# Row sums of a projection: summed on VectorE and multiplied by ones, in a two-block attention kernel on one core

## What is computed

```
# first block: softmax attention, D = 64
q = einsum('bcn,dc->bnd', x, Wq) + bq
k = einsum('bcn,dc->bdn', ctx, Wk) + bk
v = einsum('bcn,dc->bdn', ctx, Wv) + bv
x = einsum('bcm,bnm->bcn', v, softmax(q @ k)) + x
# second block: no softmax, CI = 256
g_x     = conv1x1(g_w, g_b, ctx)^T
theta_x = conv1x1(theta_w, theta_b, x)^T
phi_x   = conv1x1(phi_w, phi_b, ctx)
W = theta_x @ phi_x / 1024
wy = conv1x1(w_w, w_b, (W @ g_x)^T)
out = bn_gamma * (wy - bn_mean) / sqrt(bn_var + eps) + bn_beta + x
```

## Time and profile before

| | |
|---|---|
| Time, median of 3 runs | 1041.94 us (1041.92 to 1042.0) |
| Span of the profiled execution | 1041.2 us, first to last instruction |
| Median less span | 0.7 us |
| Granted TensorE clock | 1.000 |
| Busy: TensorE, VectorE, ScalarE, GpSimd | 99%, 62%, 47%, 26% |
| Instructions | 13910 |

### The profile page before, as it was taken

One profiled execution on the slowest core, in us unless ns is written; L12 is line 12 of the kernel. 1 busy time (PEld: TensorE's weight loads), 2 busy tenths in 40 slices (PEclk: granted clock), 3 DMA queues, 4 the chain that ended last, 5 costly groups with the idle time before them and its releaser, 6 DMA issues.

```text
span 1041.2 us, 13910 instructions
## 1 busy us (share of the span) xinstructions
PE 1032.8 (99%) x5119; PEld 854.6 (82%) x5119; DVE 647.8 (62%) x923; ACT 490.6 (47%) x843; POOL 274.9 (26%) x235
## 2 busy tenths in 40 slices
PE   8999999999999999999999999999999999999998
PEld 6778888888888887888878888888887888878887
DVE  6994467844588355873558736586365863658625
ACT  7652564436553264533744337453275532655321
POOL 1312351122601236012350124401244012430220
DMA  7536152451424524245242442434433344323512
GB/s 253 162 75 204 63 196 49 106 190 62 162 56 108 181 67 157 61 111 173 81 142 68 112 166 91 132 76 111 158 109 114 82 121 143 123 101 81 130 33 82
DMA packets 80915, 122.06 MB, mean 117 GB/s; under 512 B 13136, under 2 KB 46672, under 8 KB 80848
## 3 DMA queue, kind: packets, MB, share of 16 engines
q1 hardware_dynamic: 71632, 104.39, 32.9%
q10 hardware_dynamic: 9216, 16.78, 5.1%
HBM read 70.79 MB, written 16.78 MB: 84 GB/s over the span
## 4 chain that ended last, share of the span: by engine, by line
PE 95%; DVE 2%; SPq 1%; DMA 1%; ACT 1%; issue 0%; DVEq 0%; ACTq 0%
PE pG L651 34%; PE pG L546 15%; PE pG L662 8%; PE pG L554 5%; PE pG L587 5%; PE pT L684 4%; PE pG L684 4%; PE pG L561 4%; PE pT L493 3%; PE pS L599 2%; PE pS L482 2%; PE pM L630 2%; PE pM L639 2%; PE pT L599 2%; SPq L396 1%; PE pG L567 1%
## 5 line engine op out<-in xcount | busy, mean ns | idle before, releaser
L651 PE MATMUL pG<-pt,vT 128*128 128x512 f32 x1536 | 353.9, 389 | 0.0
L651 PEld LDWEIGHTS pG<-pt,vT 128*128 128x128 f32 x1536 | 286.8, 188 | 58.6
L1063 POOL TENSOR_TENSOR xms<-xr,xms 128x512 fp32r<-128x512 f32 x64 | 89.7, 1401 | 324.6 <-ACT xms L840 324.6
L546 PE MATMUL pG<-wv,x2s 128*128 128x512 f32 x720 | 168.6, 391 | 0.0
L546 PEld LDWEIGHTS pG<-wv,x2s 128*128 128x128 f32 x720 | 134.0, 188 | 30.3 <-issue 2.6
L996 DVE SCALAR_TENSOR_TENSOR xr<-pG,cl,xr 128x512 f32<-128x512 f32 x64 | 47.9, 749 | 170.2 <-PE pG L651 170.2
L840 ACT ACTIVATE xms<-xr 128x512 fp32r<-128x512 f32 x64 | 40.3, 629 | 178.5 <-DVE xr L996 178.5
L967 DVE TENSOR_TENSOR pt<-mv,pt 128x512 fp32r<-128x512 f32 x128 | 90.2, 756 | 39.5 <-ACT pt L811 39.3
L1059 POOL TENSOR_TENSOR ys<-yf,ys 128x256 fp32r<-128x256 f32 x32 | 28.9, 906 | 295.5 <-ACT ys L802 295.5
L811 ACT ACTIVATE pt<-mv 128x512 fp32r<-128x512 f32 x128 | 71.9, 620 | 37.5 <-PE pM L639 27.9
L662 PE MATMUL pG<-xms,wth 128*128 128x512 f32 x384 | 88.3, 389 | 0.0
(11 more groups left out here) (138 smaller groups left out, 1433.7 us busy)
## 6 DMA issues: line engine op xcount, KB each, us to landing
mv<-tp SPq DMA_DIRECT2D x512, 64.0 KB, 2.0
x2T_f<-in_ctx2T_dram SPq DMA_DIRECT2D x32, 512.0 KB, 4.8
xr<-in_x_dram ACTq DMA_DIRECT2D x64, 256.0 KB, 4.6
st<-in_ctx_dram SPq DMA_DIRECT2D x31, 512.0 KB, 5.5
st<-in_x_dram SPq DMA_DIRECT2D x29, 512.0 KB, 4.0
out_dram<-oh SPq DMA_DIRECT2D x32, 256.0 KB, 2.2
out_dram<-xr SPq DMA_DIRECT2D x31, 256.0 KB, 7.7
x_raw<-in_x_dram SPq DMA_DIRECT2D x3, 512.0 KB, 8.0
```

The lines of the kernel that those rows point to most:

```text
L546: last = mm(bank, x2s[:, l, c, 128 * m:128 * m + 128], wv[:, r, c, :], start=(c == 0 and n == 0), stop=(c == 3 and n == 2))
L651: last = mm(bank, vT[:, l, m, 128 * c:128 * c + 128], pt(h)[:, r, m, :], start=(m == 0 and n == 0), stop=(m == 7 and n == 2))
L1063: done(tt(xms(h)[:, c, LO, :], xr[c][:, :], xms(h)[:, c, HI, :].bitcast(F), ALU.subtract), "xlo")
```

## The change

The projection that is added as a term of rank one becomes that of phi, not of g, so that it is needed as a row that is the same on all partitions. It is made in three steps.

1. `acc` (blocks 1 to 7, VectorE): `acc = 8 phi_b + sum over c and part of wpg[:, part, c, 0:256] * scol[:, c]`, eight scalar_tensor_tensor of 256 columns, each of which waits for the one before. In block 0 the same is done on GpSimd, which has a tensor_scalar and a tensor_tensor for each of the eight, and one tensor_scalar for the bias.
2. `acc` on ScalarE makes the HI part, `accl` on VectorE (GpSimd in block 0) the LO part.
3. `psi` (TensorE): two matmuls with a 128 by 128 matrix of ones add up the 128 partitions, which leaves the row in all of them, in `pM[:, 1, 256:512]`. ScalarE copies it to `psi_row` after Y:3, and `mt` multiplies it by the column of g_b.

`s`, `gs`, `gt`, `gsum` and their tiles go. `Y` is made with phi_w^T (the first 256 columns of `wpg`) and phi_b. In `M` the operands change sides: `wpg` is loaded and `ys` moves. `mtf` and `mts` are moved to the place of `gram` and `xms0`; `T:4` therefore waits for `M:1`, and the evacuation PV:0,3 for `B:1`. In the strings of blocks 1 to 7 `T:4` stands ahead of `mts` and `T:5` ahead of PV:0,0, on ScalarE and VectorE, and `tr:7` ahead of `mt`. In block 0 the copy of `w_w` waits for `psi`, since the tiles of the sum lie at its place.

```diff
 LATER = dict(
     pe=(
-        "k:0 k:1 q:0 q:1 v:0 v:1 gs v:2 S:0 S:1 L:0 L:1 L:2 gt S:2 S:3 L:3 G:0 G:1 G:2 GT:0 G:3 GT:1 S:4 S:5 v:3 "
+        "k:0 k:1 q:0 q:1 v:0 v:1 psi v:2 S:0 S:1 L:0 L:1 L:2 S:2 S:3 L:3 G:0 G:1 G:2 GT:0 G:3 GT:1 S:4 S:5 v:3 "
...
+        psi_row = at("psi_row", [128, 256], F, rd + 8192)
+        mtf = at("mtf", [128, 2, 256], F, rd + 10240)
+        mts = at("mts", [128, 2, 2, 256], R, rd + 12288)
...
-                        last = mm(bank[:, 0:256], gram[:, l, d, 128 * c:128 * c + 128], wpg[:, r, d, 256:512],
+                        last = mm(bank[:, 0:256], gram[:, l, d, 128 * c:128 * c + 128], wpg[:, r, d, 0:256],
...
-            def do_gs(b):
-                eng.wait_ge(s_wlo, W_PG + 1)
-                wait(eng, "slo", b)
+            def do_psi(b):
+                wait(eng, "acclo", b)
                 if b:
                     wait(eng, "Blo", b - 1, 1)
                 else:
+                    eng.wait_ge(s_ones, 1)
                     wait_free(eng, b, 3)
-                for c in range(4):
-                    for part in (HI, LO):
-                        last = mm(pM[0:2, 1, 256:512], sst[:, c, :], wpg[:, part, c, 256:512],
-                                  start=(c == 0 and part == HI), stop=(c == 3 and part == LO))
-                done(last, "s_row")
...
+                    wait(eng, "GTlo", b, 1)
+                for part in (HI, LO):
+                    last = mm(psi_bank, ones_r[:, :], accs(b)[:, part, :], start=(part == HI), stop=(part == LO))
+                done(last, "psi")
...
-                        last = mm(pM[:, k, 0:256], ys[:, l, c, 128 * k:128 * k + 128], wpg[:, r, c, 0:256],
+                        last = mm(pM[:, k, 0:256], wpg[:, l, c, 256 + 128 * k:384 + 128 * k], ys[:, r, c, :],
...
+            def do_acc(b):
+                wait(eng, "acc", b, 7)
+                done(act(accs(b)[:, HI, :], acc(b)[:, :], ACT.Copy), "acchi")
...
                 if t == 4:
-                    wait(eng, "B", b, 1)
+                    wait(eng, "M", b, 1)
...
+            def do_acc(b):
+                wait(eng, "x2sum", b, 3)
+                eng.wait_ge(s_br8, 1)
+                for n in range(8):
+                    c, part = divmod(n, 2)
+                    if n:
+                        wait(eng, "acc", b, n - 1)
+                    done(stt(out=acc(b)[:, :], in0=wpg[:, part, c, 0:256].bitcast(F), scalar=scol[:, c:c + 1],
+                             in1=acc(b)[:, :] if n else br[:, 256:512], op0=ALU.mult, op1=ALU.add), "acc")
...
+            def do_acc(b):
+                wait(eng, "x2sum", b, 3)
+                eng.wait_ge(s_wlo, W_PG + 1)
...
+                    eng.tensor_scalar(accp[:, :], wpg[:, part, c, 0:256].bitcast(F), scol[:, c:c + 1], None,
+                                      ALU.mult).then_inc(s_accp, 1)
+                    eng.wait_ge(s_accp, n + 1)
+                    done(tt(acc(b)[:, :], accp[:, :], acc(b)[:, :] if n else br[:, 256:512], ALU.add), "acc")
```

More of the change, by code:

```diff
@@ L572, in do_GT @@
                 wait_free(eng, b, use_g(b, r))
-                if r == 0:
-                    wait(eng, "s_colc", b)
                 for c in range(r + 1, 4):
@@ L708, in do_w @@
                 eng.wait_ge(s_wd[i], 16)
+                if i == W_O:
+                    wait(eng, "psi", 0)
                 act(w_split(i, HI), W_RAW[i], ACT.Copy).then_inc(s_whi, 1)
@@ L793, in do_G @@
                 wait_free(eng, b, use_g(b, r))
+                if b and r >= 2:
+                    wait(eng, "psi", b)
                 done(act(gram[:, HI, r, G_FROM[r]:512], gram_f[r][:, G_FROM[r]:512], ACT.Copy), "Ghi")
@@ L797, in do_GT @@
                 wait(eng, "GT", b, r)
+                if b:
+                    wait(eng, "psi", b)
                 done(act(gram[:, HI, r + 1:4, 128 * r:128 * r + 128], gram_turned(r), ACT.Copy), "GThi")
@@ L812, in do_T @@
                 done(last, "Thi")
-            def do_gs(b):
-                wait(eng, "qlo", b)
-                wait(eng, "s_row", b)
-                done(act(grow, pM[0:2, 1, 256:512], ACT.Copy), "s_rowc")
-            def do_gt(b):
-                wait(eng, "s_col", b)
-                done(act(gsc[:, :, :], pM[:, 0, 384:388].rearrange("p (k i) -> p k i", i=2), ACT.Copy), "s_colc")
             def do_mts(b):
@@ L839, in do_PV @@
                 wait_free(eng, b, G_PV + 4 * h + c)
+                if h == 0 and c == 3:
+                    wait(eng, "B", b, 1)
                 done(act(xms(h)[:, c, HI, :], xr[c][:, :], ACT.Copy), "xhi")
@@ L849, in _ @@
             do = dict(w=do_w, xr=do_xr, x2=do_x2, x2a=do_x2a, xs=do_xs, x1=do_x1, k=do_k, q=do_q, k2=do_k2, q2=do_q2, v=do_v, S=do_S, L=do_L, G=do_G,
-                      GT=do_GT, Y=do_Y, x2T=do_x2T, s=do_s, T=do_T, gs=do_gs, gt=do_gt, mts=do_mts, B=do_B, xc=do_xc, PV=do_PV,
+                      GT=do_GT, Y=do_Y, x2T=do_x2T, acc=do_acc, psi=do_psi, T=do_T, mts=do_mts, B=do_B, xc=do_xc, PV=do_PV,
                       th=do_th)
@@ L970, in do_mt @@
             def do_mt(b):
-                wait(eng, "s_colc", b)
                 wait(eng, "M", b, 1)
-                if b == 0:
-                    eng.wait_ge(s_nbg, 1)
+                wait(eng, "psirow", b)
                 for k in range(2):
-                    done(stt(out=gsum[:, k:k + 1], in0=gsc[:, k, 0:1], scalar=nbg[:, k:k + 1], in1=gsc[:, k, 1:2],
-                             op0=ALU.add, op1=ALU.add), "gsum")
-                for k in range(2):
-                    wait(eng, "gsum", b, k)
-                    done(stt(out=mtf[:, k, :], in0=br[:, 0:256], scalar=gsum[:, k:k + 1], in1=pM[:, k, 0:256],
+                    done(stt(out=mtf[:, k, :], in0=psi_row[:, :], scalar=gb(k), in1=pM[:, k, 0:256],
                              op0=ALU.mult, op1=ALU.add), "mtf")
@@ L1051, in do_x2T @@
                 done(tt(x2Ts[:, LO, m, :], x2T_raw(b, m), x2Ts[:, HI, m, :].bitcast(F), ALU.subtract), "x2Tlo")
-            def do_s(b):
-                wait(eng, "shi", b)
-                done(tt(sst[:, :, LO], scol[:, :], sst[:, :, HI].bitcast(F), ALU.subtract), "slo")
+            def do_acc(b):
+                wait(eng, "x2sum", b, 3)
+                eng.wait_ge(s_wlo, W_PG + 1)
+                eng.wait_ge(s_bd, 16)
+                eng.tensor_scalar(br[:, 256:512], br[:, 0:256], N / 128.0, None, ALU.mult).then_inc(s_br8, 1)
+                eng.wait_ge(s_br8, 1)
+                for n in range(8):
+                    c, part = divmod(n, 2)
+                    if n:
+                        wait(eng, "acc", b, n - 1)
+                    eng.tensor_scalar(accp[:, :], wpg[:, part, c, 0:256].bitcast(F), scol[:, c:c + 1], None,
+                                      ALU.mult).then_inc(s_accp, 1)
+                    eng.wait_ge(s_accp, n + 1)
+                    done(tt(acc(b)[:, :], accp[:, :], acc(b)[:, :] if n else br[:, 256:512], ALU.add), "acc")
+                wait(eng, "acchi", b)
+                done(tt(accs(b)[:, LO, :], acc(b)[:, :], accs(b)[:, HI, :].bitcast(F), ALU.subtract), "acclo")
             def do_Y(b, c):
```

69 lines of the change are left out of this document (36 added, 33 removed), and 18 rows, old and new, of tables (act, dve, pe).

## The result

| | before | after |
|---|---|---|
| Time, median | 1041.97 us (1041.92 to 1042.54) | 1053.16 us (1052.74 to 1054.57) |
| Ratio | | 1.0107, 95% interval 1.0094 to 1.0119 |
| Span of the profiled execution | 1041.2 us | 1050.9 us |
| Start of k in block 1 | 140.5 us | 146.7 us |
| Mean length of a block, start of block 1 to start of block 7 | 128.24 us | 128.76 us |

What follows compares the result with a forecast made beforehand. TensorE was taken as the bound, busy 1032.8 of 1041.2 us. Block 0's cost of 1.0 less 5.3 gained in blocks 1 to 7 gave -4.3 us, so 1037.6 us, with range 1035.6 to 1040.4.

Steps and rivals of the forecast that it cites:

- TensorE's work, blocks 1 to 7: TensorE, blocks 1 to 7: matmuls 0.70 us less and small transposes 0.21 less, a gain of 0.91 us a block.
- stall in blocks 1 to 7: TensorE before S:0, blocks 1 to 7: waits 0.15 us a block because VectorE's sum delays q.
- block 0: Block 0: GpSimd's sum and its operations alongside VectorE's cost 1.0 us in all, at least 0.3, at most 3.5.
- the meeting: VectorE's sum, blocks 1 to 7: running beside GpSimd's x2T:0 split costs 0.9 us once a block.
- the upper bound of 62: GpSimd, block 0: latest end of the sum, taken to end at 58, with bounds 53.5 and 62 us.
- block 0 pays in full: Rival, chance 0.10: GpSimd's sum ends at 62, TensorE starts Y 3.5 us late, whole kernel 1040.1 us.
- a first Y after 64: TensorE, block 0: first Y expected near 62.6 us; a start after 64 would show the forecast wrong.
- VectorE's chain: VectorE, blocks 1 to 7: eight dependent sum steps ahead of k, 0.50 us each, 4.9 us with GpSimd's interference.
- Who waits: Blocks 1 to 7: q comes 1.35 us later, q2 0.79 later, so S:0 is what waits, 0.15 us.
- a block that shortens by under 0.5: Blocks 1 to 7: each expected 0.76 us shorter; under 0.5 would show the forecast wrong.
- The second half: Second half of a block: T:4 and T:5 ahead of mts and PV:0,0 cost nothing, about 1.4 us cover staying.
- The one on the slower side: Rival, chance 0.05: VectorE's sum at 0.60 us a step, stall 1.25 us a block, whole kernel 1045.3 us.

Runs made afterwards that it cites:

- e13: e11 with GpSimd's x2T:0 in blocks 1 to 7 waiting until VectorE's eight sum steps are done; 1036.61 us, ratio 0.9949 to the kernel before.
- e10: The changed kernel with 352 bytes of small tiles put ahead of the weights, restoring the old operand distance; 1045.97 us, ratio 1.0038 to the kernel before.
- e12: The kernel before with only 352 bytes of padding between the weights and all later tiles; 1052.11 us, ratio 1.0096.
- e11: e10 with, in block 0 alone, ScalarE's copy of the sum behind T:2 and TensorE's psi behind Y:2; 1040.7 us, ratio 0.9981 to the kernel before.

## Why the prediction was wrong, point by point

Two steps of the prediction failed. It put the moved tiles at nothing: they cost 6.7 us here, and it had no term for them. And it took GpSimd's tensor_scalar at 0.4 us, where the median was 1.24, so that block 0 cost 6.2 us and not 1.0. The difference between forecast and result splits into terms that the profiled spans bear. The forecast was 4.3 below the span of before, and it came out 9.7 above, 14.0 apart.

| term | forecast | measured | share of the miss |
|---|---|---|---|
| TensorE's work, blocks 1 to 7 | -0.91 a block | -0.91, of which e13 shows 0.88 | 0.2 |
| stall in blocks 1 to 7 | 0.15 a block | 0.43 (0.88 in e13 less 0.45 in e10) | 2.0 |
| block 0 | 1.0 | 6.2 | 5.2 |
| distance of the operands | no term | 6.7 (1050.9 - 1044.2), 0.98 a block, beside the stall | 6.7 |

They add up to 14.1; the starts are rounded to 0.1. How the miss is divided depends on the order in which the terms are taken away. The row of the stall is what e10 shows, with the distance repaired; in the changed kernel itself the slower products cover the stall from block 2 on, and the distance alone costs 1.3 a block (e12). And 0.4 of block 0's 6.2 are its slower B and th.

**TensorE's part: right.** 0.93 became 0.23, the 0.21 of the transposes is gone, M kept its 1.43. Undisturbed blocks of e13 are 0.94 shorter.

**The distance: a step that was missing.** "Y and M keep their number and their 256 columns, only the operands change places, so they cost nothing" was right of Y and M. But the change in the tiles' table was read only for which tile lies over which, for waits, and not for where the tiles behind it come to lie. No row of the trace of before could have given its price. A sign of it was in the diff all the same: 512 bytes in and 160 out between two sides whose operands meet in five kinds of products. It is the largest term, but it doesn't turn the sign by itself: with the old distance (e10) the kernel is still some 4 us slower, with the new one 11.2. Only when block 0 is repaired as well (e11) is it faster, by 1.8, and with the meeting gone too (e13) by 5.3.

**Block 0: the price of GpSimd's tensor_scalar.** This term failed by size, and the bound with it. It was taken at 0.4 us, "nearer to the cast". Measured in the changed kernel (min/median/max ns):

```profile
L1075 POOL TENSOR_SCALAR accp<-wpg,scol x8: 924/1242/1763, 45.5 to 61.5; 128x256 f32<-128x256 f32 x8
```

It is three times the estimate, and dearer than the tensor_tensor with two inputs beside it (line 1078, 738 median). Part of that is the meeting with VectorE, but the least is still 924, and the bias' one, with a constant in place of the column, took 865. The Trainium skill (GPSIMD Engine Reference, section 4.1) calls one-input work on GpSimd roughly line-rate, and two-input work about twice as slow as on VectorE; by these rows the form with one tensor input is not the cheaper, and the measurement decides. A pair took 2.2 us, not 1.22, and the sum ended at 63.20, later than the upper bound of 62. The rival "block 0 pays in full" had the right mechanism and stopped at 3.5 us. It also left out two things that come on top: the sum's own copy and split (0.42 and 0.73) once nobody has anything else to do, and the clock, which fell during 5.35 us of idle time and made the 36 matmuls of Y 1.4 us longer (6.27 against the 4.91 of the earlier trace rows). Its own sign of being wrong, a first Y after 64, came true at 65.90.

**VectorE's chain: right in its sum.** It should end 4.9 us after wy's last operation. Timeline of VectorE after, block 2:

```profile
276.06 0.75 DVE L1031 SCALAR_TENSOR_TENSOR xr<-pG,acol,xr 128x512 f32<-128x512 f32 x1 [0.62 <-PE pG L684]
276.73 0.47 DVE L903 SCALAR_TENSOR_TENSOR acc<-wpg,scol,br 128x256 f32<-128x256 f32 x1
277.24 4.52 DVE L903 SCALAR_TENSOR_TENSOR acc<-wpg,scol,acc 128x256 f32<-128x256 f32 x7
281.68 1.79 DVE L917 SCALAR_TENSOR_TENSOR pM<-pS,cl,k 64x256 f32<-64x256 f32 x4
```

wy's ends at 276.81, k's additions start at 281.68: 4.87. A step is 0.49 with a gap of 0.02, where 0.46 and 0.04 were forecast: the two errors cancel, which is luck. The meeting happened once a block, as forecast, at 0.9 to 1.1 us, but for block 1, which has a second one.

**Who waits: wrong place.** The forecast followed q's delay to q2, k2 and S:0 and found 0.15. It left out the split of v:0, which stands right behind q's additions on VectorE and frees v:2's bank. The rows of before had the numbers: that split ended at 280.46 and v:2 started at 282.38 in the timeline, a slack of 1.92, of which the shorter psi takes 0.70. With q 1.35 later the slack is gone and v:2 is 0.13 late. Measured, the split ends 12.17 us after wy's last operation in e10 (287.91 against 275.74) and 10.76 before (280.46 against 269.70): 1.41 later, as good as forecast. That makes 0.19 late, and v:2 starts 0.05 after the split's end: 0.25, as measured. Its twelve matmuls take another 0.11 longer. By the starts, k to S:0, the seven blocks of e10 lose 0.48 each on the mean against e13 (0.75 in block 1, 0.35 to 0.47 in the others); the 0.43 of the table is less, since e13 has its own wait in block 3. The view of waits, with 1.2 us in all, shows less than half of it. The prediction's other sign of being wrong, a block that shortens by under 0.5, came true as well, in e10 for this reason.

**The second half: right.** It costs nothing that can be measured and gives nothing.

**The rivals.** None of the four was it. The one on the slower side had a chain that is too long on VectorE as its mechanism; that chain was as short as forecast. (The 0.04 us between two VectorE operations, 289.30 to 290.09, is cited from rows 5 and stands in rows 3.)

## What to carry to other kernels

When a tile is added to or taken from a table of SBUF addresses, look at which matmuls take their two operands from different sides of it, and keep the distance, here to a multiple of 256 bytes (0 and 256 were free, 32, 64, 128, 320 and 352 were not); compare the durations of the untouched products before any other reading. Price a new operation on an engine by a row of the same kind, and where there is none, let the range reach to the dearest neighbour, and put its consumer where a miss costs nothing: here a place two steps later in block 0 was worth 5.3 us. Where work of VectorE with two SBUF inputs stands in front of something tight, let GpSimd start after it: one wait gave most of the 3.5 us between e11 and e13, the version that beats both kernels (1036.61 us). And read a short wait of TensorE from the starts of its matmuls, since the view of waits can hide 0.16 us of each.
